# Combine weights of a mixture of experts: gated dispatch matrices on GpSimd in place of distances and clipped lines on ScalarE

## The reference, cut to what matters

```
dispatch, combine = _gating_top2(logits, C)
expert_inputs = einsum('GSEC,GSM->EGCM', dispatch, x)
hidden = gelu(expert_inputs @ w0) * (expert_inputs @ w1)       # 1368 wide
expert_outputs = hidden @ wo
out = einsum('EGCM,GSEC->GSM', expert_outputs, combine)
```

## Time and profile before

| what | us |
|---|---|
| median of 3 runs | 530.7 |
| lowest and highest run | 528.23, 535.4 |
| the profiled execution, its time | 534.06 |
| its span, first to last instruction | 531.9 |

### The profile page before, as it was taken

The page is one execution under the profiler, slowest core; times in us unless marked ns, Lnnn a source line. Parts: engine busy times, 40 slices in busy tenths (PEclk is TensorE's granted clock), DMA queues, the critical chain, the costliest instruction groups (busy, mean ns, idle before and its releaser), DMA issues.

```text
span 531.9 us, 18452 instructions
## 1 busy us (share of the span) xinstructions
PE 494.0 (93%) x6699; PEld 453.6 (85%) x6699; DVE 390.4 (73%) x988; ACT 338.3 (64%) x870; POOL 270.7 (51%) x360
## 2 busy tenths in 40 slices
PE   1897999999999999999998779998999999999997
PEld 0776889888889888888886668998999999999996
DVE  2544536666666758667678988978889999999984
ACT  1445676666757757667674256789866676666651
POOL 4134442544435454453644273877856666667660
PEclk9977999999999999999999997999999999999999
DMA  6614111111111111011003700555464666365402
GB/s 173 186 52 116 26 27 46 36 44 24 42 42 22 38 40 40 20 40 20 3 4 77 245 2 0 171 153 200 139 211 133 194 194 192 127 199 176 144 1 80
DMA packets 58126, 48.92 MB, mean 92 GB/s; under 512 B 20942, under 2 KB 49744, under 8 KB 58064
## 3 DMA queue, kind: packets, MB, share of 16 engines
q1 hardware_dynamic: 58064, 48.09, 31.0%
HBM read 46.86 MB, written 1.08 MB: 90 GB/s over the span
## 4 chain that ended last, share of the span: by engine, by line
PE 77%; issue 5%; ACT 5%; DMA 5%; DVE 4%; SPq 2%; POOL 1%; ACTq 0%; DVEq 0%; POOLq 0%
PE bank L225 20%; PE bank L227 18%; PE bank L226 18%; PE bank L646 5%; PE bank L614 3%; PE bank L667 3%; ACT Pr L1149 2%; PE bank L571 2%; DMA ctx_raw<-in_ctx 2%; DMA w_raw<-in_L_xattn_Wk 2%; PE bank L1045 1%; DMA last_prob<-Pr 1%; SPq L426 1%; PE bank L803 1%; PE bank L924 1%
## 5 line engine op out<-in xcount | busy, mean ns | idle before, releaser
L225 PE MATMUL bank<-XT_lo,W_hi 128*128 128x256 f32 (+1 forms) x352 | 99.3, 282 | 0.2 <-DVE XT_lo L1927 0.2
L226 PE MATMUL bank<-XT_hi,W_lo 128*128 128x256 f32 (+1 forms) x352 | 99.0, 281 | 0.0
L227 PE MATMUL bank<-XT_hi,W_hi 128*128 128x256 f32 (+1 forms) x352 | 98.7, 281 | 0.0
L2324 POOL TENSOR_TENSOR W_lo<-raw,W_hi 128x256 fp32r<-128x256 f32 (+1 forms) x88 | 83.8, 953 | 7.0
L2217 POOL TENSOR_TENSOR Pr<-Pr,rinv 128x1028 f32<-128x1028 f32 (+2 forms) x32 | 60.5, 1891 | 49.4 <-DVE rinv L1509 48.7
L1149 ACT ACTIVATE Pr<-Sc,nmax 128x257 f32<-128x257 f32 x128 | 63.8, 502 | 25.4 <-DVE nmax L1498 17.5
L1498 DVE CUSTOM_DVE_ANT_0 Sc<-bank,mask_add 128x257 f32<-128x257 f32 x128 | 47.0, 423 | 41.3 <-PE bank L614 18.0
L1971 DVE TENSOR_TENSOR W_lo<-raw,W_hi 128x512 fp32r<-128x512 f32 (+1 forms) x88 | 71.3, 811 | 4.9 <-ACT W_hi L1316 1.2
L2322 POOL CAST W_hi<-raw 128x256 fp32r<-128x256 f32 (+1 forms) x88 | 43.1, 489 | 58.5 <-PE bank L227 36.7
L2144 DVE TENSOR_TENSOR hid_lo<-hid,hid_hi 128x256 fp32r<-128x256 f32 (+1 forms) x88 | 67.5, 767 | 1.5 <-ACT hid_hi L1403 1.5
L225 PEld LDWEIGHTS bank<-XT_lo,W_hi 128*128 128x128 f32 (+1 forms) x352 | 65.4, 186 | 0.4 <-issue 0.4
(11 more groups left out here) (250 smaller groups left out, 1374.0 us busy)
## 6 DMA issues: line engine op xcount, KB each, us to landing
raw<-in_L_ffn_w_kernel SPq DMA_DIRECT2D x32, 512.0 KB, 4.6
ctx_raw<-in_ctx SPq DMA_DIRECT2D x32, 256.0 KB, 2.8
raw<-in_L_ffn_wo_kernel SPq DMA_DIRECT2D x16, 512.0 KB, 5.7
raw<-in_L_ffn_w_kernel SPq DMA_DIRECT2D x16, 344.0 KB
last_prob<-Pr SPq DMA_DIRECT2D x128, 1.0 KB, 1.8
raw<-in_L_ffn_wo_kernel SPq DMA_DIRECT2D x8, 256.0 KB
x_sb<-in_x SPq DMA_DIRECT2D x4, 256.0 KB, 6.2
VL_all<-vl_rows SPq DMA_DIRECT2D x8, 128.0 KB
```

Of the source, the lines that this page charges most:

```text
L225: pe.matmul(dst, a_hi, b_lo, start=first, stop=False)
L226: pe.matmul(dst, a_lo, b_hi, start=False, stop=False)
L227: return pe.matmul(dst, a_hi, b_hi, start=False, stop=last)
L2324: po.tensor_tensor(W2_lo[0:w, m % RW, :], raw2[0:w, t, :], f(W2_hi[0:w, m % RW, :]), ALU.subtract)\
```

## The change

`disp` is kept through the expert stage, and GpSimd makes `C_all` from it: once, `gate_experts` multiplies `chosen` by `gate` (repeated over the experts) and adds the two choices, which gives `gates_of`, 128 x 8 tiles x 8 experts; then `weigh(t)` multiplies the dispatch matrix of tile t by it, each gate repeated over 32 slots. ScalarE's part and `negate_gates` go. `C_all` now shares its place with `y_hi`, and `far` and `second_of` are gone.

```diff
+    weighed = ExitStack()
+    C_all = sb("C_all", [P, TT, E * CAP], scope=weighed)
+    weighed.close()
     y_hi = sb("y_hi", [P, TT, D], F32R)
...
-    C_all = sb("C_all", [P, TT, E * CAP])
-    past, gate, less_gate = (sb(n, [P, 2, TT]) for n in ("past", "gate", "less_gate"))
+    disp = sb("disp", [P, TT, E * CAP], F32R)
+    past, gate = (sb(n, [P, 2, TT]) for n in ("past", "gate"))
+    gates_of = sb("gates_of", [P, TT, E])
...
-    disp = sb("disp", [P, TT, E * CAP], F32R, early)
...
-    far, second_of = sb("far", [P, E * CAP]), sb("second_of", [P, E * CAP])
...
 # ScalarE
-        def weigh(t, c):
-
-            ac.wait_ge(sm["tail_left"], 2)
-            if t + c > 0:
-                ac.wait_ge(sm["w_act"], 4 * t + 2 * c)
-            ac.activation(far[:, :], slot_no, ACT.Abs, bias=past[:, c, one(t)], scale=-1.0).then_inc(sm["w_act"], 1)
-            ac.wait_ge(sm["w_act"], 4 * t + 2 * c + 1)
-            if c == 1 and t > 0:
-                ac.wait_ge(sm["r_weighed"], t)
-            ac.activation((C_all[:, t, :], second_of[:, :])[c], far[:, :], ACT.Relu, bias=gate[:, c, one(t)],
-                          scale=less_gate[:, c, one(t)]).then_inc(sm["w_act"], 1)
...
-            if WEIGH_AT <= m < WEIGH_AT + 2 * TT:
-                weigh(*divmod(m - WEIGH_AT, 2))
 # VectorE
-                mark(("gates", t), ve.tensor_scalar(gate[:, 1, one(t)], gate[:, 1, one(t)], gate[:, 0, one(t)], None, ALU.mult))
+                gates = ve.tensor_scalar(gate[:, 1, one(t)], gate[:, 1, one(t)], gate[:, 0, one(t)], None, ALU.mult)
+                if t == TT - 1:
+                    gates.then_inc(sm["tail_left"], 1)
...
-        def negate_gates():
-            need(("gates", TT - 3), ("gates", TT - 2), ("gates", TT - 1))
-            ve.tensor_scalar(less_gate[:, :, :], gate[:, :, :], -1.0, None, ALU.mult).then_inc(sm["tail_left"], 1)
...
-        negate_gates()
 # GpSimd
-        def add_weights(t):
-
-            po.wait_ge(sm["w_act"], 4 * t + 4)
-            po.tensor_tensor(C_all[:, t, :], C_all[:, t, :], second_of[:, :], ALU.add).then_inc(sm["r_weighed"], 1)
+        def gate_experts():
+
+            po.wait_ge(sm["tail_left"], 2)
+            po.tensor_tensor(chosen[:, :, :, :], chosen[:, :, :, :], gate[:, :, :].unsqueeze(3).broadcast_to([P, 2, TT, E]), ALU.mult)\
+              .then_inc(sm["gates_made"], 1)
+            po.wait_ge(sm["gates_made"], 1)
+            po.tensor_tensor(gates_of[:, :, :], chosen[:, 0], chosen[:, 1], ALU.add).then_inc(sm["gates_made"], 1)
+
+        def weigh(t):
+
+            po.wait_ge(sm["gates_made"], 2)
+            own, placed = (a.rearrange("p (e c) -> p e c", c=CAP) for a in (C_all[:, t, :], f(disp[:, t, :])))
+            po.tensor_tensor(own, placed, gates_of[:, t, :].unsqueeze(2).broadcast_to([P, E, CAP]), ALU.mult).then_inc(sm["r_weighed"], 1)
...
-            if m - WEIGH_AT - 6 in range(0, 2 * TT, 2):
-                add_weights((m - WEIGH_AT - 6) // 2)
+            if m == WEIGH_AT - 1:
+                gate_experts()
+            if m - WEIGH_AT in range(0, 2 * TT, 2):
+                weigh((m - WEIGH_AT) // 2)
```

More of the change, by code:

```diff
@@ L206, in program @@
         b_oT_made b_oT_hi b_oT_lo b_wo_made b_x2
-        c_bn c_mv c_var c_r c_y c_yT_made c_yT c_logits_made c_lg c_rounded c_kept r_neg t_dve ra_shifted ra_exp r_weighed w_act r_reach d_disp tail_left last_normed r_exp r_chosen r_pos_made r_disp
+        c_bn c_mv c_var c_r c_y c_yT_made c_yT c_logits_made c_lg c_rounded c_kept r_neg t_dve ra_shifted ra_exp r_weighed gates_made r_reach d_disp tail_left last_normed r_exp r_chosen r_pos_made r_disp
         r_x_made r_x_kept diag_zero
```

## The result

The changed kernel has a median of 525.44 us (523.46 to 528.14, 11 runs) beside 530.76 us (527.89 to 535.4, 11 runs) for the kernel before: 5.3 us less by the medians, ratio 0.9891, 95% interval 0.9865 to 0.9917, which is 4.4 to 7.2 us less. The forecast was 2.6 us less and 528.1 us. The direction and the range held; the forecast size was half of what was measured.

A forecast was written before the change was run, and what follows sets the result against it. TensorE bounds the kernel, with ScalarE's weigh holding it up in the expert stage. 3.1 us regained minus 0.5 of stalls gives 2.6, from the median 530.7 to 528.1 us; range 525 to 532.

The forecast's parts named there:

- rival D: Expert stage: the 2.3 us lost belong to copies of the first expert's output, not ScalarE; 530.7 us, chance 0.10.
- The forecast's own steps on GpSimd: Expert stage: GpSimd's step becomes 1.7 to 2.0 us, below 2.13; gate_experts, 0.4 to 0.85 us, is hidden.
- the place of the multiplies: GpSimd's steps 6 to 20 instead of 12 to 26: starting six steps earlier buys nothing and cannot be late.
- `negate_gates` is worth nothing: Start of the expert stage: VectorE loses this 0.70 us instruction while TensorE is fully busy; counted as 0.
- I let 0.5 us of stalls stay or come back: Expert stage, around VectorE's copies of expert outputs: 0.5 us of stalls subtracted from the gain.
- The 3.1 us of the sum: TensorE's lost time in the expert stage: 2.3 us in the weigh stretch plus at most 0.8 in the second gap.
- the tiles move in SBUF ... I take 0: C_all over y_hi, disp outside early: no wait or DMA added or removed, nothing prices an address; 0 us.
- A sign I had and didn't use: Profiled execution, 534.06 us, lay 3.4 us above the runs' median of 530.7; the same 2.6 us was taken from the median.
- Rivals B: Expert stage: each multiply costs VectorE 0.74 us, taking most of the gain back; gain 0.4, 530.3 us, chance 0.22.
- rival C: Expert stage: each multiply holds VectorE 1.19 us, making it slower, 534.0 us; decides from 0.8 us a multiply; chance 0.08.
- The forecast's argument against the whole lock: Steady expert stage: shortest VectorE and GpSimd durations end to end make 2.22 us, over the 2.13 us step without TensorE idling.

The follow-up runs named there:

- act_load_back: Changed kernel with ScalarE's 32 weighing instructions put back, read by nobody and without the wait for GpSimd; stage 191.23 us against 190.00.
- no_multiply: Changed kernel without gate_experts and the eight multiplies, transposes reading the dispatch matrices; stage 189.98 us against 190.00, ratio 0.9895 to the kernel before.
- late_multiply: Changed kernel with the multiplies in GpSimd's steps 12 to 26, where the adds were, instead of 6 to 20; stage 190.00 us.
- negate_back: Changed kernel with VectorE's negate_gates instruction put back, writing a tile nobody reads; stage 190.00 us.
- no_negate: Kernel before without negate_gates, ScalarE scaling by the gate itself; stage 193.38 us, ratio interval 1.0002 to 1.0050.
- old_layout: Changed kernel with all tiles of the opening at the SBUF addresses of the kernel before; 526.67 us, ratio 0.9944 to the kernel before.
- w_off: Changed kernel with w_raw alone moved down by 64 bytes, to an odd multiple of 64; ratio 0.9948 to the kernel before.
- layout_only: Kernel before with only its tiles placed in SBUF as in the changed kernel, ScalarE still weighing; ratio 0.9982 to the kernel before.
- double_multiply: Changed kernel with each of the eight multiplies issued twice, same result; stage 191.20 us, 1.2 over the changed kernel.
- after_again: The changed kernel itself, timed once more as a control; 527.94 us, ratio 0.9925 to the kernel before.
- all_aligned: Changed kernel with context loads ahead of the vl_rows wait, w_raw and ctx_raw at multiples of 512 bytes; as fast as with context loads ahead alone, 523.56 us.

## Why the prediction was right and wrong

**Right, and shown.** TensorE sets the pace of the stage, and `weigh` on ScalarE made it stumble: act_load_back brings the first gap back, and between the two first profiles the loss appears nowhere else in the stage. Both gaps went, against rival D; that the load made the second one too is not shown by itself. The forecast's own steps on GpSimd held: `gate_experts` and the multiplies are covered (no_multiply), the place of the multiplies doesn't matter (late_multiply), `negate_gates` is worth nothing (negate_back, no_negate).

**Too low in the stage.** The step "I let 0.5 us of stalls stay or come back" had nothing behind it: no stall came back, and the multiplies that were to make VectorE late took nothing from it (36.80 us busy without them, 36.58 with). The stage gave 3.4 us in the two profiles and 3.05 as a mean over all, against 2.6. The 3.1 us of the sum, before the 0.5 came off, are what came out.

**The step that failed** is the one that stopped at the stage. Under "the tiles move in SBUF ... I take 0" I looked for waits and found none, and under the sum I carried only the stage's microseconds to the median. Measured were 5.3 us, and 3.05 of them are the stage's. About 0.35 us lie outside the span: a run's time is 2.06 to 2.16 us over its span in every run of the kernel before and of its variants, and 1.73 to 1.82 in every run of the changed kernel and its variants, act_load_back among them. The cause of that step of 0.35 us stays open. The remaining 1.9 us lie ahead of the stage (behind it both profiles have 10.0 us). They may go with the addresses in part: old_layout and w_off, which have the changed kernel's stage and other places in the opening, reach 0.9944 and 0.9948, about what the stage and the 0.35 us make by themselves (0.994), where the changed kernel has 0.9891 and 0.9925. But these intervals overlap or nearly touch, and layout_only, which has the places alone, gained nothing that its interval (0.9954 to 1.0009) tells from zero. So the forecast's 0 for the addresses is not refuted. Some is scatter of the opening, which the repeat shows by itself: 0.9891 and 0.9925 for one and the same kernel. How the 1.9 us divide, and their cause, stay open. That the range of 525 to 532 us holds the result, by 0.4 us, is luck: it was drawn for scatter, not for a gain ahead of the stage.

**A sign I had and didn't use.** The profiled execution lay 3.4 us over its median, and I put that down as a distance to be carried along. Its likely cause was in the same trace: a write that took 3.4 us to land, a wait of 2.9 us that ended at 48 us, and half clock behind it. It did not change the forecast, which took the same 2.6 us off the median, but whoever finds the reason for such a distance also learns how much the medians will scatter.

**Rivals B and C** priced a multiply for VectorE at 0.74 and 1.19 us. Leaving the eight out gave VectorE nothing back (no_multiply), and eight more cost the kernel 0.07 us each, where rival C decided from 0.8. The rule of the Trainium skill, "SBUF — State Buffer", section "Who interferes with whom", speaks of a lock for the whole of an instruction. The trace of the changed kernel agrees that durations depend on what the other engine does (GpSimd's multiply 0.61 to 1.07 us, VectorE's `hid_lo` 0.41 to 0.96), but while neither engine was full it cost the kernel nothing.

The forecast's argument against the whole lock, 2.22 us of shortest durations in a step of 2.13, does not hold as it stands, because successive instructions of one engine overlap in these traces. Shortest from start to start, VectorE's `W_lo` and `hid_lo` take 0.60 and 0.33 us and GpSimd's `W_lo` 0.68; with 0.39 for `W_hi` that is 2.0 us, which fits in a step. double_multiply is the better test. With 0.56 us for each multiply, what ran in its 39.5 us (19, 18, 18 and 18 of these four and 14 multiplies) adds up to an estimated 44 us, so not all of it can have run one at a time. Without the `W_hi` casts it would be 37, so it may be these that the lock spares; no run here tells.

## What to carry to other kernels

Where one engine sets the pace, price an edit on another by the pace-setter's gaps (matmuls missing in a window), not by the busy time removed: 17.5 us of ScalarE's work were worth 3.05 us. Compare a helper engine's step, start to start, with the pace-setter's: 2.21 against 2.13 us was enough for a loss, once a wait and a copy came on top. Before you price a loss by a stage's length, look at the granted clock where the stage begins: half of what double_multiply seemed to cost was that. And before carrying a profile's microseconds to a median, find out why that execution is off its median; measure a stage's own length beside the total, since it repeats within 0.6 us where the total moves by 4.

## What the runs showed of the hardware that I had not expected

A write of 32 KB by one issue landed after 1.5 us in most profiles and after 3.3 to 3.7 in five of nineteen (before, after_again, no_negate, late_multiply, all_aligned), with nothing between. In three of those, before, after_again and no_negate, the granted clock of TensorE fell to half for about 7 us around the end of its wait, and they fell back by 3.7 to 4.1 us over the next matmuls; in late_multiply it did not, and 1.9 us were lost. old_layout had 3.4 us at half clock without a late write, behind a wait of 2.7 us. Instructions of ScalarE overlap: in one step of the kernel before (from 354.41 us) the five durations 0.36, 0.62, 0.42, 0.49 and 0.60 us make 2.49, but the step repeats every 2.21 us, so sums of durations overstate what ScalarE needs.
